# Keys of the cross-attention projected feature-major by head, their inverse roots applied to the scores

## The chip, the cores and the metric

The kernel runs on one core of one Trainium2 chip. The metric is the device time of one launch in microseconds (us). The kernel is written with explicit queues: each engine (PE for matmuls, DVE, ACT, POOL, and SP, which issues DMAs) has its own list of instructions and runs it in order; semaphores order the engines against each other.

## The reference

Input `x` is 16 sequences of 64 rows of 256 floats, and each sequence has a context of 64 rows of 128 floats. All data is float32 except the feed-forward weights and activations after quantising. Three blocks follow each other, each with a residual sum and a layer norm:

1. A chunked linear test-time-training attention (TTT): 16 heads of 16, four chunks of 16 steps. Each chunk needs the state that the chunk before it left, so the four chunks form a chain.
2. A cross-attention with 16 heads of 128 over the context. This is the part that the change touches:

```
q = rmsnorm((x @ Wq).reshape(.., 16, 128), gq)
k = rmsnorm((ctx @ Wk).reshape(.., 16, 128), gk)     # k * rsqrt(mean(k*k) + eps) * gk
attn = softmax(einsum(q, k) / sqrt(128));  out = (attn @ v) @ Wo
```

3. A feed-forward block with weights and activations rounded to 8-bit levels.

## The kernel before, in words

The program has three stages.

**Preparation.** Weights are loaded, transposed, quantised; `x` is transposed and projected for the TTT block; the product of value and output weights of the cross-attention is made (`mvo`).

**TTT stage with the keys between.** DVE runs the chain of four chunks (`chain`, `after_own_terms`, `out_a`, `out_b`, `out_c`, lines 1066 to 1180). PE runs for each chunk `scores_ttt` (L503), `own_terms` (L521) and `state_products` (L511), which are many matmuls of 32 rows and few columns. Between them PE does units of work on the keys of the cross-attention. There are 32 units; a unit is 128 context rows (one main tile) times 512 features (4 heads). PE projects it (L479), which gives the rows token-major. ACT takes four sums of squares (L816) and copies the unit to `kraw` (L817). POOL makes the inverse root and scales the unit (`k_scale`, L1363 to L1365). Three units later PE transposes it head by head (L487), and ACT writes it to `kt` scaled by the gain `gk` (L821). The order is written out by hand: of the units of chunk c (`KEY_UNITS[c]`), PE does the first `FIRST_UNITS[c]` before `scores_ttt(c + 1)`, those up to `EARLY_UNITS[c]` before `own_terms(c)`, and the others behind it, before `state_products(c + 1)`; units 28 to 31 and the last transposes come after the last `own_terms`. ACT has the roots of the chain (L825) between the same units, and POOL the output gating of the chain (L1374 to L1382).

`own_terms(c)` waits for the update of the chunk from DVE (`ub_ready`, L1109). When the last `own_terms` is done (`mg_done` at 8), SP loads `x` a second time (its place had been taken) and the query weights `xwq` (L345 to L348).

**Main loop.** Eight tiles of 128 rows go through a software pipeline (lines 675 to 718 for PE): in iteration i PE projects the queries of tile i (L566), transposes them (L580), makes the scores of tile i (L598, 128 rows by 64 columns of weights, alternately to the upper and lower 64 rows of the output), the context sums and the output of tile i-1 (L610, L618), and the feed-forward of tiles i-2 and i-3 (L637, L647, L655). On DVE the softmax of tile i (L1252 maximum, L1255 subtraction) stands ahead of the rounding of the hidden row of tile i-2 (L1204 to L1208), for whose transposes (`h_transpose`, L647) PE waits at the end of the iteration. The loop starts when the last `o_feat` (L1148) and the last `key_emptied` (L821) are there; its first instruction is `ttt_out` (L661).

## Time and profile before

| | |
|---|---|
| median of 3 runs | 466.35 us (463.65 to 470.18) |
| the profiled execution, span from first to last instruction | 463.8 us |
| PE busy | 373.4 us, 81% |
| DVE busy | 274.3 us, 59% |
| ACT busy | 244.4 us, 53% |
| POOL busy | 218.3 us, 47% |
| preparation, TTT stage, main loop | about 0 to 61, 61 to 207.7, 207.7 to 463.8 us |

For the profiled execution only its span is given; it lies 0.15 us above the fastest run and 2.5 us below the median. Busy shares are means over stages with different limits; what a stage is bound by is read from the waits and the chain inside it. In the slices, each digit is a fortieth of the span (11.6 us).

### The profile page before, as it was taken

The numbers are of one execution on the slowest core, as the hardware profiler recorded it, in microseconds if no ns is written. First come the engines' busy times: TensorE is split into PE (matmuls) and PEld (weight loads), VectorE is DVE, ScalarE is ACT, GpSimd is POOL, SyncE is SP. The second block draws the span as 40 slices with busy tenths as digits, with TensorE's granted clock in tenths as the row PEclk, the third lists the DMA queues.
The fourth block names the chain that finished last, engine by engine and source line by source line (L and its number), as shares of the span: only waits on it lengthen the run. The fifth ranks groups of instructions, "written<-read, shape, count | busy, mean of one in ns | idle before, by whom it ended". The sixth has DMA issues, their size and how long they took to land.

```text
span 463.8 us, 11063 instructions
## 1 busy us (share of the span) xinstructions
PE 373.4 (81%) x4570; PEld 231.0 (50%) x4570; DVE 274.3 (59%) x438; ACT 244.4 (53%) x818; POOL 218.3 (47%) x231
## 2 busy tenths in 40 slices
PE   2999967775775764648869999999999999997952
PEld 2445736444544432424536657485665748464531
DVE  1479953898798895362232427474572737446455
ACT  3036942644453567453655484857568484763320
POOL 2044898699699699761303333232334322224001
PEclk9899975977789979777989999999999999998675
DMA  8990000000000000420000000000000000000000
GB/s 265 193 349 28 0 4 4 6 3 4 3 4 3 3 1 2 171 103 0 2 0 1 0 2 2 11 1 12 2 0 13 1 12 1 11 2 0 13 0 23
DMA packets 12625, 14.54 MB, mean 31 GB/s; under 512 B 2192, under 2 KB 11808, under 8 KB 12064
## 3 DMA queue, kind: packets, MB, share of 16 engines
q1 hardware_dynamic: 12544, 13.83, 9.9%
q8 instruction: 36, 0.59, 0.5%
q14 instruction: 13, 0.11, 0.1%
q10 hardware_dynamic: 32, 0.02, 0.0%
HBM read 12.80 MB, written 1.05 MB: 30 GB/s over the span
## 4 chain that ended last, share of the span: by engine, by line
PE 41%; ACT 6%; DVE 5%; POOL 4%; issue 1%; POOLq 0%; ACTq 0%; DVEq 0%
PE ps L566 12%; PE ps L618 11%; PE ps L610 5%; PE ps L598 3%; PE ps L580 3%; PE ps L637 2%; PE ps L589 2%; PE ps L661 1%; ACT qt L881 1%; PE ps L655 1%; POOL kraw L1365 1%; ACT qjunk L871 1%; POOL krs L1364 1%; ACT cxp L902 1%; PE ps L647 1%
## 5 line engine op out<-in xcount | busy, mean ns | idle before, releaser
L566 PE MATMUL ps<-xwq,x1t 128*128 128x512 f32 x128 | 64.5, 634 | 0.9 <-ACT x1t L893 0.9
L816 ACT ACTIVATE junk<-ps 128x128 bf16<-128x128 f32 x128 | 33.9, 292 | 50.9 <-PE ps L479 50.7
L618 PE MATMUL ps<-mvo,cxp 128*128 128x256 f32 x256 | 58.8, 384 | 0.1
L618 PEld LDWEIGHTS ps<-mvo,cxp 128*128 128x128 f32 x256 | 47.9, 191 | 7.2 <-issue 0.7
L479 PE MATMUL ps<-xwk,ctxt 128*128 128x512 f32 x64 | 46.4, 823 | 0.0
L871 ACT ACTIVATE qjunk<-ps 128x128 f32<-128x128 f32 x128 | 33.4, 279 | 17.9 <-PE ps L566 17.7
L487 PEld LDWEIGHTS ps<-ident,kraw 128*128 128x128 f32 x128 | 18.8, 170 | 46.9 <-issue 23.3
L487 PE MATMUL ps<-ident,kraw 128*128 128x128 f32 x128 | 24.6, 326 | 20.3 <-POOL kraw L1365 9.6
L1365 POOL TENSOR_TENSOR kraw<-kraw,krs 128x512 f32<-128x512 f32 x32 | 36.0, 1126 | 2.5
L1364 POOL TENSOR_TENSOR krs<-krs,mhalf 128x4 f32<-128x4 f32 x32 | 35.5, 1110 | 2.7
L566 PEld LDWEIGHTS ps<-xwq,x1t 128*128 128x128 f32 x128 | 23.2, 198 | 26.6 <-issue 24.0
L1405 POOL TENSOR_SCALAR rstd<-mv 128x1 f32<-128x1 f32 x24 | 5.3, 221 | 58.5 <-DVE mv L1196 58.5
L1422 POOL TENSOR_TENSOR pr<-pr,rq 128x1024 f32<-128x1024 f32 x7 | 13.3, 1902 | 40.7 <-DVE pr L1255 40.7
L1415 POOL TENSOR_SCALAR rq<-qss 128x16 f32<-128x16 f32 x8 | 1.6, 205 | 64.6 <-ACT qtok L872 64.6
L610 PE MATMUL ps<-pt,ctx 64*128 64x512 f32 x64 | 30.2, 698 | 0.7 <-ACT pt L883 0.7
L881 ACT ACTIVATE qt<-ps,gqs 128x512 f32<-128x512 f32 x32 | 22.3, 698 | 13.7 <-PE ps L580 13.7
L816 ACT ACTIVATION_READ_ACCUMULATOR junk<-ps 128x1 f32 x128 | 28.1, 224 | 0.1
L871 ACT ACTIVATION_READ_ACCUMULATOR qjunk<-ps 128x1 f32 x128 | 27.0, 211 | 0.0
L521 PE MATMUL ps<-ak,ub 32*32 32x48 f32 (+1 forms) x1024 | 15.2, 217 | 14.0 <-issue 9.9
L1231 DVE TENSOR_TENSOR rr<-ps,xn 128x256 f32<-128x256 f32 x8 | 3.4, 425 | 38.4 <-PE ps L661 38.4
L821 ACT ACTIVATE kt<-ps,gks 128x512 f32<-128x512 f32 x32 | 23.2, 724 | 4.0 <-PE ps L487 3.9
L1238 DVE TENSOR_TENSOR gs<-ps,s 128x352 f32<-128x352 f32 x16 | 8.4, 525 | 28.5 <-PE ps L637 28.5
(214 smaller groups left out, 849.0 us busy)
## 6 DMA issues: line engine op xcount, KB each, us to landing
xn<-in_x_dram SPq DMA_DIRECT2D x4, 512.0 KB, 4.4
xwo<-in_L_xattn_Wo_dram SPq DMA_DIRECT2D x1, 2048.0 KB, 14.9
xwq<-in_L_xattn_Wq_dram SPq DMA_DIRECT2D x1, 2048.0 KB, 9.2
w1n<-in_L_ffn_w_gate_up_dram SPq DMA_DIRECT2D x1, 1408.0 KB, 9.0
ctx<-in_ctx_dram SPq DMA_DIRECT2D x2, 512.0 KB, 9.2
xwv<-in_L_xattn_Wv_dram SPq DMA_DIRECT2D x1, 1024.0 KB, 12.2
xwk<-in_L_xattn_Wk_dram SPq DMA_DIRECT2D x1, 1024.0 KB, 17.0
out_dram<-x SPq DMA_DIRECT2D x8, 128.0 KB, 1.7
```

What stands on the lines that cost most here:

```text
L479: mm(bank(bk), ctxt[:, i * P:(i + 1) * P], xwk[:, qn * BANK:(qn + 1) * BANK], start=True, stop=True)\
L487: last = nc.tensor.transpose(bank(bk, P, t * P), kraw[:, h * XD:(h + 1) * XD], ident[:, :])
L521: last = mm(ps[part, g * GW + C:g * GW + C + w], ub[part, g * 32:(g + 1) * 32], ak[part, g * (C + 32):g * (C + 32) + w], start=c == 0 and ...
L566: last = mm(bank(n % 2), x1t[:, (i % 2) * D + k * P:(i % 2) * D + (k + 1) * P], xwq[:, k * XH * XD + qn * BANK:k * XH * XD + (qn + 1) * BA ...
L610: turn_done(mm(bank(bk), ctx2[rows, b * CD:(b + 1) * CD], pt[rows, :].rearrange("p (h q) -> p h q", q=P)[:, :, b2 * T:(b2 + 1) * T], start ...
L618: last = mm(bank(6 + turn_of[("y", i, 0)] % 2, D), cxp[:, h * P:(h + 1) * P], mvo[:, h * D:(h + 1) * D], start=h == 0, stop=h == XH - 1)
L816: A(junk[:, t * P:(t + 1) * P], bank(bk, P, t * P), ACT.Square, accum_out=kss[:, h:h + 1])
L821: A(kt[:, m * BANK:(m + 1) * BANK], bank(bk), ACT.Copy, scale=gks[:, 0:1]).then_inc(sem("key_emptied"), 1)
L871: A(qjunk[:, t * P:(t + 1) * P], bank(n % 2, P, t * P), ACT.Square, accum_out=qraw_ss[:, h:h + 1])
L881: ins = A(qt[:, n * BANK:(n + 1) * BANK], src, ACT.Copy, scale=gqs[:, 0:1])
L1364: step(GP.tensor_tensor(krs[:, head], krs[:, head], mhalf[:, 0:4], ALU.pow))
L1365: GP.tensor_tensor(groups(kraw[:, own], XD), groups(kraw[:, own], XD), spread(krs[:, head], 4, XD), ALU.mult)\
```

## The change

The keys are now computed feature-major, one head at a time. A unit is one head (128 features) times 512 context rows (half of them); there are again 32 units. PE's projection has the weights of the head as the stationary side, so that no transposes are needed. ACT squares the unit into `ksq` and copies it to `kt` with the product of both gains. PE sums the squares over the features with a matmul whose stationary side is 32 one-hot columns (`key_sum`): each head adds its sums into a row of its own of PSUM bank 5, even heads in the rows of one group of 32, odd heads in the next. After 16 units ACT takes the roots of 64 rows (`key_roots`). SP writes the rows to DRAM and reads them back in another layout, DVE takes the reciprocal (`key_scales`), SP writes it to DRAM, and for each main tile SP reads a row per sequence, broadcast over the 64 partitions, into `rkb` (two DMAs per tile). In the main loop DVE multiplies the scores by `rkb`, and takes maximum and subtraction from the product. POOL's `k_scale` is gone, and so are the units behind the last `own_terms`.

Some memory moves: `ak` now lies over `ctx2`, so the context is loaded a second time after the last `own_terms`, behind `xwq` and `x`, and PE waits for it before the main loop. The amounts of units ahead of each step change (`KEY_UNITS`, `EARLY_UNITS`). The copy of the transposed queries (L881) has no gain any more.

```diff
-KEY_BANKS, KEY_LAG = 3, 3
-NKU = 4 * NT
-KEY_UNITS = [range(0, 6), range(6, 13), range(13, 20), range(20, 28)]
-TAIL_SPLIT = (2, 4)
+NKU = 2 * XH
+KEY_UNITS = [range(0, 9), range(9, 17), range(17, 25), range(25, NKU + 1)]
 FIRST_UNITS = [3, 2, 2, 2]
-EARLY_UNITS = [4, 5, 5, 8]
+EARLY_UNITS = [7, 7, 7, 8]
...
+        krow0 = place("krow0", BANK)
+        assert cursor[0] == after_kt
+        ak = place("ak", G * (C + 32), over="ctx2")
...
+        krow1 = place("krow1", BANK, over="ctxt")
...
+            def roots_to_rows(half):
+                sp.wait_ge(sem("k_rooted"), half + 1)
+                krow = (krow0, krow1)[half]
+                for odd in range(2):
+                    at = 64 * half + 32 * odd
+                    sp.dma_start(kroot[half].rearrange("b (r o) t -> o r b t", o=2)[odd],
+                                 krow[at:at + XH // 2, :].rearrange("p (b t) -> p b t", t=T)).then_inc(sem("k_rows_out"), 16)
+                sp.wait_ge(sem("k_rows_out"), 32 * (half + 1))
+                sp.dma_start(kinv[:, half * T:(half + 1) * T], kroot[half].rearrange("b h t -> (b h) t")).then_inc(sem("k_roots_in"), 16)
+
+            def scales_out(half):
+                sp.wait_ge(sem("k_inverted"), half + 1)
+                sp.dma_start(kscale[half * B // 2:(half + 1) * B // 2, :].rearrange("b (h t) -> (b h) t", t=T),
+                             kinv[:, half * T:(half + 1) * T]).then_inc(sem("k_scales_out"), 16)
+
+            def scale_rows(i):
+                sp.wait_ge(sem("k_scales_out"), 16 * (i // 4 + 1))
+                if i >= 2:
+                    sp.wait_ge(sem("s_read"), i - 1)
+                for b2 in range(2):
+                    sp.dma_start(rkb[b2 * T:(b2 + 1) * T, (i % 2) * XH * T:(i % 2 + 1) * XH * T],
+                                 kscale[2 * i + b2:2 * i + b2 + 1, :].broadcast_to([T, XH * T])).then_inc(sem("ld_rkb%d" % (i % 2)), 16)
+
+            roots_to_rows(0)
+            scales_out(0)
+            roots_to_rows(1)
             sp.wait_ge(sem("mg_done"), 2 * NCH)
+            load(xwq[:, :].rearrange("p (k n) -> p k n", k=KT), XWq.rearrange("(k p) n -> p k n", p=P), "xwq")
             load_x()
-
-            load(xwq[:, :].rearrange("p (k n) -> p k n", k=KT), XWq.rearrange("(k p) n -> p k n", p=P), "xwq")
+            for half in range(2):
+                load(ctx2[half * T:(half + 1) * T, :].rearrange("p (b c) -> p b c", c=CD), ctx_in.rearrange("b s c -> s b c"), "ctx")
+            sp.wait_ge(sem("k_summed"), NKU)
+            scale_rows(0)
+            scale_rows(1)
+            scales_out(1)
             o = out.rearrange("b t d -> (b t) d")
-            for i in range(NT):
-                sp.wait_ge(sem("x3_ready"), i + 1)
-                sp.dma_start(o[i * P:(i + 1) * P, :], x3[:, (i % 2) * D:(i % 2 + 1) * D]).then_inc(sem("stored%d" % (i % 2)), 16)
+            for i in range(NT + 3):
+                if i >= 3:
+                    t = i - 3
+                    sp.wait_ge(sem("x3_ready"), t + 1)
+                    sp.dma_start(o[t * P:(t + 1) * P, :], x3[:, (t % 2) * D:(t % 2 + 1) * D]).then_inc(sem("stored%d" % (t % 2)), 16)
+                if i + 2 < NT:
+                    scale_rows(i + 2)
...
+            def key_sum(n):
+                half, h = n // XH, n % XH
+                rows = slice(64 * half + 32 * (h % 2), 64 * half + 32 * (h % 2) + 32)
+                pe.wait_ge(sem("k_squared"), n + 1)
+                at = 31 - h // 2
+                mm(bank(5)[rows, :], onehot[:, at:at + 32], ksq[:, (n % 2) * BANK:(n % 2 + 1) * BANK],
+                   start=h < 2, stop=h >= XH - 2).then_inc(sem("k_summed"), 1)
 
...
                 if n < NKU:
-                    i, qn = n // 4, n % 4
-                    bk = key_bank("project", n)
-                    mm(bank(bk), ctxt[:, i * P:(i + 1) * P], xwk[:, qn * BANK:(qn + 1) * BANK], start=True, stop=True)\
+                    half, h = n // XH, n % XH
+                    if n >= 2:
+                        pe.wait_ge(sem("key_emptied"), n - 1)
+                    mm(bank(6 + n % 2), xwk[:, h * XD:(h + 1) * XD], ctxt[:, half * BANK:(half + 1) * BANK], start=True, stop=True)\
                         .then_inc(sem("key_done"), 1)
-                m = n - KEY_LAG
-                if m >= 0:
-                    bk = key_bank("transpose", m)
-                    pe.wait_ge(sem("k_scaled"), m + 1)
-                    for t in range(4):
-                        h = m % 4 * 4 + t
-                        last = nc.tensor.transpose(bank(bk, P, t * P), kraw[:, h * XD:(h + 1) * XD], ident[:, :])
-                    last.then_inc(sem("key_done"), 1)
+                if n >= 2 and n % 2 == 0:
+                    key_sum(n - 2)
+                    key_sum(n - 1)
...
-            for n in range(KEY_UNITS[-1].stop, NKU + KEY_LAG):
-                key_unit(n)
...
-            pe.wait_ge(sem("key_emptied"), len(key_turns))
+            pe.wait_ge(sem("key_emptied"), NKU)
+            pe.wait_ge(sem("k_rooted"), 2)
+            pe.wait_ge(sem("ld_ctx"), 64)
...
+            A(gks[:, 1:2], gks[:, 0:1], ACT.Copy, scale=gqs[:, 0:1]).then_inc(sem("gains"), 1)
...
+            def key_roots(half):
+                act.wait_ge(sem("k_summed"), (half + 1) * XH)
+                rows = slice(64 * half, 64 * half + 64)
+                A((krow0, krow1)[half][rows, :], bank(5)[rows, :], ACT.Sqrt, bias=eps_t[rows, 1:2], scale=1.0 / XD)\
+                    .then_inc(sem("k_rooted"), 1)
...
             def key_unit(n):
...
-                    bk = key_wait("project", n)
-                    if n >= 1:
-                        act.wait_ge(sem("key_emptied"), key_of[("project", n - 1)] + 1)
-                    if n >= 4:
-                        act.wait_ge(sem("key_done"), key_of[("transpose", n - 4)] + 1)
-                    for t in range(4):
-                        h = n % 4 * 4 + t
-                        A(junk[:, t * P:(t + 1) * P], bank(bk, P, t * P), ACT.Square, accum_out=kss[:, h:h + 1])
-                    A(kraw[:, n % 4 * BANK:(n % 4 + 1) * BANK], bank(bk), ACT.Copy).then_inc(sem("key_emptied"), 1)
-                m = n - KEY_LAG
-                if m >= 0:
-                    bk = key_wait("transpose", m)
-                    A(kt[:, m * BANK:(m + 1) * BANK], bank(bk), ACT.Copy, scale=gks[:, 0:1]).then_inc(sem("key_emptied"), 1)
+                    half, h = n // XH, n % XH
+                    act.wait_ge(sem("key_done"), n + 1)
+                    if n >= 2:
+                        act.wait_ge(sem("k_summed"), n - 1)
+                    A(ksq[:, (n % 2) * BANK:(n % 2 + 1) * BANK], bank(6 + n % 2), ACT.Square).then_inc(sem("k_squared"), 1)
+                    if n == XH + 12:
+                        act.wait_ge(sem("k_rows_out"), 32)
+                    o = kt[:, :].rearrange("p (i h t) -> p h i t", h=XH, t=P)[:, h, half * 4:half * 4 + 4]
+                    A(o, bank(6 + n % 2).rearrange("p (i t) -> p i t", t=P), ACT.Copy, scale=gks[:, 1:2]).then_inc(sem("key_emptied"), 1)
+                if n >= XH and n % XH == 0:
+                    key_roots(n // XH - 1)
...
-            rest = range(KEY_UNITS[-1].stop, NKU + KEY_LAG)
-            for n in rest[:TAIL_SPLIT[0]]:
-                key_unit(n)
             root_of(ovs, osd, "ovs_ready", 2 * NCH - 1, "osd_ready")
-            for n in rest[TAIL_SPLIT[0]:TAIL_SPLIT[1]]:
-                key_unit(n)
             root_of(ovs, osd, "ovs_ready", 2 * NCH, "osd_ready")
-            for n in rest[TAIL_SPLIT[1]:]:
-                key_unit(n)
...
-                    ins = A(qt[:, n * BANK:(n + 1) * BANK], src, ACT.Copy, scale=gqs[:, 0:1])
+                    ins = A(qt[:, n * BANK:(n + 1) * BANK], src, ACT.Copy)
...
+                if c == 0:
+                    dve.wait_ge(sem("job_done"), index_of[("ctxt", (1,))] + 1)
...
+            def key_scales(half):
+                dve.wait_ge(sem("k_roots_in"), 16 * (half + 1))
+                own = slice(half * T, (half + 1) * T)
+                V.reciprocal(kinv[:, own], kinv[:, own]).then_inc(sem("k_inverted"), 1)
...
+                if c >= NCH - 2:
+                    key_scales(c - (NCH - 2))
...
                     dve.wait_ge(sem("sc_done"), i + 1)
-                    step(V.tensor_reduce(mx[:, :], groups(s, T), AX.X, ALU.max))
+                    dve.wait_ge(sem("ld_rkb%d" % (i % 2)), 32 * (i // 2 + 1))
                     if i >= 2:
                         dve.wait_ge(sem("tp_done"), tp_of[("pt", i - 2, 1)] + 1)
-                    V.tensor_tensor(groups(z, T), groups(s, T), spread(mx[:, :], XH, T), ALU.subtract).then_inc(sem("s_read"), 1)
+                    V.tensor_tensor(z, s, rkb[:, (i % 2) * XH * T:(i % 2 + 1) * XH * T], ALU.mult).then_inc(sem("s_read"), 1)
+                    dve.wait_ge(sem("s_read"), i + 1)
+                    step(V.tensor_reduce(mx[:, :], groups(z, T), AX.X, ALU.max))
+                    V.tensor_tensor(groups(z, T), groups(z, T), spread(mx[:, :], XH, T), ALU.subtract).then_inc(sem("s_shifted"), 1)
                     if i == 0:
-                        dve.wait_ge(sem("s_read"), 1)
+                        dve.wait_ge(sem("s_shifted"), 1)
                         dve.wait_ge(sem("rq_ready"), 1)
                         V.tensor_tensor(groups(z, T), groups(z, T), spread(rq[:, :], XH, T), ALU.mult).then_inc(sem("z_ready"), 1)
...
+            step(GP.memset(onehot[:, :], 0.0))
+            GP.memset(onehot[:, 31:32], 1.0).then_inc(sem("mask_parts"), 1)
...
-            def k_scale(n):
-                own = slice(n % 4 * BANK, (n % 4 + 1) * BANK)
-                head = slice(n % 4 * 4, (n % 4 + 1) * 4)
-                pool.wait_ge(sem("key_emptied"), key_of[("project", n)] + 1)
-                step(GP.tensor_scalar(krs[:, head], kss[:, head], 1.0 / XD, RMS_EPS, ALU.mult, ALU.add))
-                step(GP.tensor_tensor(krs[:, head], krs[:, head], mhalf[:, 0:4], ALU.pow))
-                GP.tensor_tensor(groups(kraw[:, own], XD), groups(kraw[:, own], XD), spread(krs[:, head], 4, XD), ALU.mult)\
-                    .then_inc(sem("k_scaled"), 1)
...
-                for n in KEY_UNITS[c][:EARLY_UNITS[c]]:
-                    k_scale(n)
...
-                for n in KEY_UNITS[c][EARLY_UNITS[c]:]:
-                    k_scale(n)
-            rest = range(KEY_UNITS[-1].stop, NKU)
-            for n in rest:
-                k_scale(n)
...
-                    pool.wait_ge(sem("s_read"), i + 1)
+                    pool.wait_ge(sem("s_shifted"), i + 1)
```

## Rows read from the trace of the kernel before

**Rows 1.** The page, part 2: granted clock of PE in 40 slices, tenths.
```profile
PEclk9899975977789979777989999999999999998675
```
**Rows 2.** Waits, 60 to 208 us, DVE: total us, times, longest.
```profile
DVE qhR L1113 <- PE ps L521: 15.9, 5, 8.3
DVE ogt L1148 <- POOL oR L1382: 3.6, 2, 2.4
```
**Rows 3.** The page, part 5: busy, mean ns | idle before. POOL's key work.
```profile
L1365 POOL TENSOR_TENSOR kraw<-kraw,krs 128x512 f32<-128x512 f32 x32 | 36.0, 1126 | 2.5
```
**Rows 4.** Line L479: duration ns min/median/max, first and last start us.
```profile
L479 PE MATMUL ps<-xwk,ctxt x64: 592/697/1222, 62.8 to 197.3; 128*128 128x512 f32 x64
```
**Rows 5.** Timeline of PE: start, us, line, count [idle before <-releaser].
```profile
75.96 2.08 PE L479 MATMUL ps<-xwk,ctxt 128*128 128x512 f32 x2
77.83 1.06 PE L487 MATMUL ps<-ident,kraw 128*128 128x128 f32 x4
78.82 4.27 PE L521 MATMUL ps<-ak,ub 32*32 32x48 f32 x256
...
108.99 1.22 PE L521 MATMUL ps<-ak,ub 32*32 32x48 f32 x97 [1.84 <-DVE ub L1109]
...
144.24 2.16 PE L521 MATMUL ps<-ak,ub 32*32 32x48 f32 x177 [2.14 <-DVE ub L1109]
...
182.69 1.13 PE L521 MATMUL ps<-ak,ub 32*32 32x16 f32 x112
```
**Rows 6.** Windows: us, busy of PE, PEld, DVE, ACT, POOL, PEclk, DMA share, GB/s.
```profile
71.00:81.00 10.00, 8.29 (x352) 6.67 (x344) 2.13 (x4) 2.21 (x10) 7.83 (x11) 0.50 0.02 5
```
**Rows 7.** Timeline of PE: four passes of 512 columns; 64 passes of 64 columns.
```profile
291.57 1.88 PE L566 MATMUL ps<-xwq,x1t 128*128 128x512 f32 x4
...
303.35 2.08 PE L598 MATMUL ps<-kt,qt 128*64 128x64 f32 x64
```
**Rows 8.** Line L1101, min/median/max: a DVE step of the chain, with and without POOL.
```profile
L1101 DVE TENSOR_TENSOR uR<-dd,rn x3: 691/1411/1411, 105.2 to 174.8; 128x512 f32<-128x512 f32 x3
```
**Rows 9.** Timelines of PE and DVE in chunk 3.
```profile
168.20 1.11 PE L487 MATMUL ps<-ident,kraw 128*128 128x128 f32 x4 [4.45 <-ACT kraw L817]
...
178.28 0.71 DVE L1109 STREAM_TRANSPOSE ub<-ubt 128x512 f32<-128x512 f32 x1
```
**Rows 10.** Timelines of DVE and PE from the last own terms to the main loop.
```profile
190.48 0.45 DVE L1113 STREAM_TRANSPOSE qhR<-ps 128x256 f32<-128x256 f32 x1 [3.75 <-PE ps L521]
...
197.00 0.35 DVE L1137 RECIPROCAL ors<-osd 128x32 f32<-128x32 f32 x1 [2.55 <-ACT osd L825]
...
204.72 0.71 DVE L1148 STREAM_TRANSPOSE ogt<-oR 128x512 f32<-128x512 f32 x1
...
207.68 3.54 PE L661 MATMUL ps<-wo,ogt 128*128 128x256 f32 x8 [0.87 <-ACT kt L821]
```
**Rows 11.** DMA issues: KB each, median us to landing; last row: `ctx` alone.
```profile
xwq<-in_L_xattn_Wq_dram SPq DMA_DIRECT2D x1, 2048.0 KB, 9.2
ctx<-in_ctx_dram SPq DMA_DIRECT2D x2, 512.0 KB, 9.2
out_dram<-x SPq DMA_DIRECT2D x8, 128.0 KB, 1.7
...
DMA to landing us min/median/max: 7.9/9.2/10.5
```
**Rows 12.** Windows, as in rows 6: the second load of `x` and `xwq`.
```profile
193.00:200.00 7.00, 5.83 (x24) 2.76 (x22) 4.24 (x7) 7.00 (x37) 5.42 (x8) 0.94 1.04 408
```
**Rows 13.** Timelines of DVE and PE in main tiles 0 and 3.
```profile
237.65 1.50 PE L589 MATMUL ps<-ident,pr 128*128 128x128 f32 x8 [4.18 <-DVE pr L1270]
...
308.47 1.22 DVE L1255 TENSOR_TENSOR pr<-ps,mx 128x1024 f32<-128x1024 f32 x1
...
312.15 0.53 DVE L1208 TENSOR_SCALAR hq<-gs 128x704 bf16<-128x704 f32 x1
...
312.74 0.63 PE L647 MATMUL ps<-ident_b,hq 128*128 128x128 bf16 x6
```

48 lines of the change are left out of this document (20 added, 28 removed).

## The prediction

> **What bounds the kernel now.** I read the clock by slice first, then the waits of DVE, then the timelines of PE and DVE stage by stage. From slice 22 on the clock is full until the last tiles, and in the TTT stage (slices 6 to 18) it wavers between seven and nine tenths [rows 1], since PE pauses there. So there are two regimes. In the TTT stage DVE runs the chain of four chunks, and what holds it is mostly PE's `own_terms`: 15.9 us of waits, of which 8.3 in chunk 0; POOL holds it for 3.6 us [rows 2]. In the main loop PE sets the pace, unless a result that it needs comes late. One is on the edge: in tile 3 the rounded hidden row ends at 312.68 (312.15 + 0.53) and PE's transposes of it start at 312.74 [rows 13]; the same pair of rows stands so in each of tiles 2 to 5, and with 0.36 us to spare in tile 6. This edge and the stretch between the last update and the main loop decide the case; the shares of busy time don't.
>
> **What POOL's relief is worth.** `k_scale` vanishes, 36.0 us in its scaling alone [rows 3]. POOL is no bound, so this counts only where it held others. A DVE step of the chain takes 691 or 1411 ns, and the long ones lie beside a POOL instruction [rows 8]. Beside key instructions lie one such step in chunk 1 on the way to the update (0.7 us), one in chunk 2 (0.7), and 1.2 us in chunk 3; behind `own_terms(2)` there are 1.3 us more, and about 1.8 us of the wait for the gated output [rows 2], which then starts without a key unit ahead of it.
>
> **What the key units cost on PE.** Before, a unit was one product of 512 columns (two passes) and four transposes, 2.08 and 1.06 us at half clock (a pass takes 592 ns at the full level of 2.4 GHz and up to 1222 at 1.2) [rows 4, 5]. Passes of 512 columns follow each other every 0.47 us at full clock (1.88 / 4) [rows 7], with the key pattern's small gaps 0.51, so a product is 1.02. After, a unit has one product and one one-hot sum, also 512 columns. The trace has no such sum. Its nearest row is L598, whose weights of 64 columns write alternately to two halves of the output: 64 passes of 64 columns in 2.08 us, where the rate of L566 would give 3.8 (4096 x 0.92 ns) [rows 7]. So two column groups overlap. A pair of sums (four passes) costs 1.02 us if all overlap, 2.04 if none do. I take 1.43, three pass slots, since passes start in order and the second sum's first pass can only lie beside the first sum's last. Two units are then 3.5 us of PE against 3.3 before.
>
> After L598 PE goes on with full-width weights with no gap above 0.1 us in the timeline, so I price the change of shape at 0. The Trainium skill (TensorEngine Tiling (Array Packing), Key Properties) says instead that changing the tiling mode drains the engine, which speaks against a scheme that changes it twice for each of 16 pairs; by that rule with 0.2 us for a drain, an estimate, the stage would be up to 6 us longer, and most of that would lie ahead of `own_terms`. It belongs to the slower rival below.
>
> **Chunk by chunk**, the shift of `own_terms` against before:
> - Chunk 0. Before, unit 3 alone stood ahead: 75.96 to 78.82, at half clock [rows 5, 6], with the update long there. Now units 3 to 6: four products and two pairs, 4 x 1.02 + 2 x 1.43 = 6.9 us of full-speed work. The clock stays at half to about 81.2 as before, where the window at 0.50 ends [rows 6], in which 5.2 us do 2.6 of it; the other 4.3, with gaps of 0.3, end at 85.8. Shift +7.0 (bounds +4.4, all at full clock, and +8.2, no overlap).
> - Chunk 1. DVE's update comes at +7.0 - 0.7. PE has five units ahead (five products, two pairs, 8.3 us) against 7.0 us for three units before, plus 2.6 for a half-clock stretch as long as the one there. So PE ends last: +8.6 on 108.99 [rows 5]. Behind it stands one unit instead of two, -0.6.
> - Chunk 2. The same count ahead: +8.9 on 144.24. Behind it DVE ends last, with 3.2 us less (the relief above, less 0.5 for the new reciprocal): the state is read at +5.7.
> - Chunk 3. The update, before at 178.3, comes at +5.7 - 1.2 = 182.8. Units 26 to 31 wait, as before [rows 9], for ACT, which stands at a root of the chain; from there 9.2 us of units and 2.5 for the half clock give 185.3 against 182.69 before, which POOL paced. Shift **+2.6**, bounds -1 (update alone) and +5.
>
> **From the last own terms to the main loop.** Before: SP issues the loads at 190.5, and the main loop starts at 207.7 [rows 10], 17.2 us, held by the last key units. These go. Then two things race. DVE's tail was 190.48 to 205.43; without the key units on ACT ahead of the root the wait of 2.55 becomes the usual 0.39, one step loses 0.7 of contention, and the reciprocal adds 0.5: 12.8 us. The loads: `xwq` and `x` ran at 408 GB/s with the DMAs full [rows 12] and ended 10.2 us after `own_terms` (issued 1.0 later, 9.2 to landing [rows 11]). The context adds 1 MB behind them in 512 B pieces. In the preparation its halves were issued 0.7 us apart and took 7.9 and 10.5 to landing [rows 11], so the second ended 3.3 after the first, and the first 2.6 after the transfer ahead of it. That makes +5.9: 16.1 us. Bounds 12.8 (1 MB at 408 GB/s is 2.5 us) and 17.5. So the context takes the place of the key tail, and **1.1 us** of 17.2 are gained.
>
> The reciprocal of the second half waits for a trip through DRAM: root 0.9 us after the last unit, two writes and a read issued at 0.5 each, two landings of 1.7 [rows 11], 5.5 us in all. Covered by `own_terms(3)`, which takes 7.7; if it took the 4.3 of chunk 0 [rows 5], DVE would wait 1 us, and the context would still hide it. SP has its wait for those writes ahead of the big loads, done some 3 us before they are due. In the main loop the rows for tile i+2 are asked for when tile i's scores are read, over 27 us ahead of need, and stores wait behind them for nothing later; cost 0.
>
> **Main loop.** DVE gets one more instruction of 128x1024 per tile, 1.22 us [rows 13], 1.26 with its hand-over. In tiles 2 to 5 it lies in front of the rounding, whose chain has no slack: 4 x 1.26, in tile 6 0.9. In tile 0 PE waits for the softmax as it is (4.18 us [rows 13]), and in tile 7 too: 2 x 1.26. Tile 1 has 1.3 us to spare: 0.1. Sum 8.6. The copy of the queries without a gain takes 0.61 instead of 0.69 and stands on the path once per tile or twice: -0.8. So **+7.8**; bounds 2.7 (tiles 2 to 6 hidden) and 10.
>
> **Sum.** 463.8 + 2.6 - 1.1 + 7.8 = 473.1 us of span. The page's span lies at the fastest run and 2.5 us below the median; I put the median at 474.
>
> **Rivals.**
> 1. Slower: sums that do not overlap or that drain PE, at half clock. Place: ahead of `own_terms`. Each pair costs 0.6 to 1 us more; two pairs ahead in chunks 0 to 2, three behind the root in chunk 3; some 8 pairs, 5 to 8 us, nearly doubled while the clock is at 1.2 GHz, less what DVE's slack takes. It decides from where `own_terms` starts right behind a sum rather than behind the update. For it: the clock [rows 6]; against it L598. 473.1 + 7 = 480.
> 2. Faster: denser PE work keeps the clock up (for it: the old half-clock stretches follow pauses; against it: those pauses are the small matmuls, which stay). Then the update alone holds chunk 3 at -1 to -3, and the context comes with the first bound: 473.1 - 5 - 2.5 = 465.5.
> 3. The multiplication is hidden, since ACT and DVE drift apart from PE by a tile: 473.1 - 5 = 468. Against it: four tiles show the same 0.06 us.
> 4. The roots don't come in time (the trip is longer than its cover), so DVE waits ahead of `out_a(3)` and the tail starts late: each us beyond 2 counts once the context is passed; 477. Little for it.
> 5. Much faster, under 457: needs 2 and 3 together and more.
>
> **Chances.** Forecast (470 to 476) 0.40, rival 1 0.22, rival 2 0.15, rival 3 0.10, rival 4 0.06, rival 5 0.07. The time is 474, the range 462 to 482. A measurement here tells about 2% from no change, 457 to 475.7. The forecast lies across the upper bound, nearer inside: two thirds of it, rivals 2, 3 and a third of 4 count as same, 0.54; rival 1, the rest of the forecast and of 4 as slower, 0.39; faster 0.07.
>
> **What would show it.** In the timeline of PE: pairs of sums in 1.4 us at full clock; `own_terms` at about 86, 118, 153 and 185. The main loop's first product behind a wait for the context, about 209. Between the last output product of tile i-1 and the transposes of the hidden row (tiles 2 to 5) an idle time of about 1.2 us with DVE as releaser, and a tile period of 28.3 instead of 27.1. I am wrong if `own_terms(3)` starts before 181, if the loop starts behind `o_feat` and not the context, or if the period stays at 27.1.

## The result, and the profile after

The changed kernel takes 468.19 us (median of 4 runs, 467.75 to 468.77) against 465.39 us (463.65 to 470.18), ratio 1.0128 [1.0083, 1.0173]: somewhat slower, within the 2%. The ratio is that of the fast runs; the plain quotient of the two medians is 1.006. 474 was forecast with a range of 462 to 482. The profiled run has a span of 466.3 us (time 468.09), 2.5 over the 463.8 of before, where 473.1 was forecast. In the four runs of the changed kernel the span is 1.7 to 1.9 us shorter than the time of the same run; so a span should not be compared with other runs' times, as it was when the median was forecast, and 473.1 us of span stands for about 475 of time. The small difference hides two large movements of opposite sign, which the positions of `own_terms` and of the loop show (us in the span; the loop's start is the first product of `ttt_out`):

| | own 0 | own 1 | own 2 | own 3 | loop start | last scores | span |
|---|---|---|---|---|---|---|---|
| before | 78.8 | 109.0 | 144.2 | 182.7 | 207.7 | 411.1 | 463.8 |
| forecast | 85.8 | 117.6 | 153.1 | 185.3 | 209.2 | | 473.1 |
| after | 82.6 | 114.7 | 145.0 | 175.4 | 199.6 | 409.8 | 466.3 |

The loop starts 8.1 us earlier, not 1.5 later, and then takes 266.7 us instead of 256.1, not 263.9. Of the 8.1, 1.75 were there already in the preparation, which has no work on the keys (the first scores of the TTT stage started 1.75 earlier; the first 16 products of the preparation took 7.1 us instead of 8.8, a half-clock stretch being shorter).

The clock by slice, from the page. Against [rows 1], counting slices from 0: higher in slices 6, 8 to 10, 14 and 18, lower in 13 and 15, and 0.5 in slices 16 and 17, where it was 0.7.
```profile
PEclk9999977988889787559899999999999999996685
```
Windows (columns as [rows 6]), first before, from `own_terms(0)` to `own_terms(3)` chunk by chunk:
```profile
78.82:108.99 30.17, 22.16 (x811) 15.15 (x811) 25.31 (x33) 18.47 (x79) 24.28 (x24) 0.85 0.01 4
108.99:144.24 35.25, 24.02 (x811) 16.28 (x811) 29.46 (x41) 16.30 (x74) 29.63 (x30) 0.81 0.01 3
144.24:182.69 38.45, 24.59 (x572) 14.68 (x572) 31.68 (x44) 22.10 (x102) 33.10 (x36) 0.87 0.01 2
```
and after:
```profile
82.60:114.68 32.08, 25.03 (x804) 12.18 (x803) 25.56 (x36) 12.01 (x21) 7.57 (x5) 0.89 0.01 3
114.68:144.96 30.28, 23.32 (x801) 11.60 (x800) 25.83 (x37) 10.48 (x21) 10.63 (x7) 0.89 0.03 6
144.96:175.37 30.41, 24.12 (x549) 9.89 (x549) 27.06 (x42) 11.39 (x22) 8.26 (x6) 0.83 0.01 4
```
PE is busy 1.7 us more than before, POOL 60 us less in the three. DVE runs the same chain in 8.0 us less busy time, all of it in the second and third, and sits idle 3.1 us less. Its waits after, 57 to 200 us, answer to [rows 2]:
```profile
DVE qhR L1145 <- PE ps L555: 15.6, 3, 12.8
DVE ogt L1180 <- POOL oR L1417: 2.5, 2, 1.2
```
The wait for own terms has the same sum, but now 12.8 of it in chunk 0. The steps of the chain that ran beside POOL are at their short time, where [rows 8] had 1411:
```profile
L1133 DVE TENSOR_TENSOR uR<-dd,rn x3: 691/691/692, 108.1 to 171.7; 128x512 f32<-128x512 f32 x3
```
The timeline of PE after. L518 is the product of a unit, L508 the sum of squares, x4 being two units, a pair of heads; L555 `own_terms`, L693 `ttt_out`, L679 the transposes of the hidden row in tile 3. It answers to [rows 5, 10, 13].
```profile
80.57 1.12 PE L518 MATMUL ps<-ctxt,xwk 128*128 128x512 f32 x2 [0.27 <-ACT kt L856]
81.62 1.05 PE L508 MATMUL ps<-ksq,onehot 128*32 128x512 f32 x4
82.60 1.63 PE L555 MATMUL ps<-ak,ub 32*32 32x48 f32 x130
...
173.57 1.87 PE L508 MATMUL ps<-ksq,onehot 128*32 128x512 f32 x4
175.37 1.50 PE L555 MATMUL ps<-ak,ub 32*32 32x16 f32 x152
179.01 1.06 PE L555 MATMUL ps<-ak,ub 32*32 32x16 f32 x104 [2.13 <-issue]
199.61 3.75 PE L693 MATMUL ps<-wo,ogt 128*128 128x256 f32 x8 [19.54 <-DMA ctx<-in_ctx_dram]
...
303.84 3.62 PE L650 MATMUL ps<-mvo,cxp 128*128 128x256 f32 x16
308.70 0.63 PE L679 MATMUL ps<-ident_b,hq 128*128 128x128 bf16 x6 [1.24 <-DVE hq L1247]
```
Four things to see: a pair of sums takes 1.05 us at full clock (1.92 at half clock, at 151.47) and the full-width products on both sides follow without a gap; `own_terms(3)` follows right behind a pair, which takes 1.87 us although the clock is full, since its second sum starts at 174.39 only, when ACT has squared the last unit (below); the loop stands 19.5 us behind a DMA; and PE waits 1.24 us for the hidden row, as forecast. ACT ahead of that pair's second sum:
```profile
173.74 0.60 ACT L852 ACTIVATE ksq<-ps 128x512 f32<-128x512 f32 x1
```
On DVE in tile 3:
```profile
301.91 1.23 DVE L1294 TENSOR_TENSOR pr<-ps,rkb 128x1024 f32<-128x1024 f32 x1
...
308.12 0.53 DVE L1247 TENSOR_SCALAR hq<-gs 128x704 bf16<-128x704 f32 x1
```
SP's queue behind the last own terms, start and time of each issue:
```profile
180.12 0.40 SPq L318 DMA_DIRECT2D xwq<-in_L_xattn_Wq_dram  x1
180.56 2.54 SPq L318 DMA_DIRECT2D xn<-in_x_dram  x2
183.15 6.30 SPq L318 DMA_DIRECT2D ctx<-in_ctx_dram  x2
189.56 5.60 SPq L366 DMA_DIRECT2D rkb<-kscale  x4
```
The engines meanwhile (columns as [rows 6], the last three PEclk, DMA share and GB/s):
```profile
180.00:208.00 28.00, 6.93 (x20) 3.98 (x14) 13.85 (x26) 1.03 (x3) 2.06 (x5) 0.51 0.74 190
```
DVE had the last features written at 191.95; PE waits 7.7 us beyond that, and its clock is at the lower level, 1.2 GHz.

### The profile page after: what moved, and what is told of

It is laid out like the page before. It is cut to its first block, busy times and chain, and to the rows that moved or that the text cites. A ratio compares the mean times of both kernels' runs of the same rounds, so it can differ in the third digit from the quotient of the medians.

```text
span 466.3 us, 10600 instructions
## 1 busy us (share of the span) xinstructions
PE 371.8 (80%) x4506; PEld 214.4 (46%) x4506; DVE 276.9 (59%) x448; ACT 210.1 (45%) x565; POOL 134.2 (29%) x137
## 3 DMA queue, kind: packets, MB, share of 16 engines
q1 hardware_dynamic: 16768, 19.27, 15.3%
## 4 chain that ended last, share of the span: by engine, by line
PE 46%; DVE 26%; ACT 8%; POOL 7%; issue 6%; DMA 4%; SPq 2%; POOLq 0%; DVEq 0%; ACTq 0%
PE ps L598 12%; PE ps L642 5%; PE ps L429 4%; PE ps L518 4%; PE ps L650 3%; DMA ctx<-in_ctx_dram 3%; PE ps L612 3%; PE ps L508 2%; PE ps L621 2%; SPq L318 2%; DVE pr L1294 2%; DVE mx L1296 2%; DVE pr L1297 2%; PE ps L669 2%; ACT sg L942 2%
## 5 line engine op out<-in xcount | busy, mean ns | idle before, releaser
L518 PE MATMUL ps<-ctxt,xwk 128*128 128x512 f32 x64 | 45.6, 829 | 4.4 <-ACT kt L856 3.5
L852 ACT ACTIVATE ksq<-ps 128x512 f32<-128x512 f32 x32 | 19.1, 596 | 61.1 <-PE ps L518 33.4
L901 ACT ACTIVATE qjunk<-ps 128x128 f32<-128x128 f32 x128 | 33.6, 281 | 16.1 <-PE ps L598 15.9
L911 ACT ACTIVATE qt<-ps 128x512 f32<-128x512 f32 x32 | 19.2, 602 | 14.7 <-PE ps L612 14.7
L693 PE MATMUL ps<-wo,ogt 128*128 128x256 f32 x32 | 9.9, 447 | 19.5 <-DMA ctx<-in_ctx_dram 19.5
L518 PEld LDWEIGHTS ps<-ctxt,xwk 128*128 128x128 f32 x64 | 13.4, 243 | 25.8 <-issue 14.4
L1444 POOL TENSOR_TENSOR rq<-rq,mhalf 128x16 f32<-128x16 f32 x8 | 23.3, 2910 | 0.7
L612 PEld LDWEIGHTS ps<-ident,qtok 128*128 128x128 f32 x128 | 15.4, 141 | 16.4 <-issue 13.0
L923 ACT ACTIVATE x1t<-ps 128x256 f32<-128x256 f32 x8 | 3.1, 384 | 42.7 <-PE ps L701 42.7
L932 ACT ACTIVATE cxp<-ps 128x512 f32<-128x512 f32 x32 | 18.9, 628 | 6.9 <-PE ps L642 6.9
L537 PE MATMUL ps<-kq,kb 32*32 32x16 f32 x1024 | 11.4, 186 | 12.3 <-issue 10.0
## 6 DMA issues: line engine op xcount, KB each, us to landing
xwv<-in_L_xattn_Wv_dram SPq DMA_DIRECT2D x1, 1024.0 KB, 12.8
```

Source lines behind the costliest of these rows:

```text
L518: mm(bank(6 + n % 2), xwk[:, h * XD:(h + 1) * XD], ctxt[:, half * BANK:(half + 1) * BANK], start=True, stop=True)\
L612: last = nc.tensor.transpose(bank(bk, P, t * P), qtok[:, (n % 2) * BANK + t * P:(n % 2) * BANK + (t + 1) * P], ident[:, :])
L852: A(ksq[:, (n % 2) * BANK:(n % 2 + 1) * BANK], bank(6 + n % 2), ACT.Square).then_inc(sem("k_squared"), 1)
L901: A(qjunk[:, t * P:(t + 1) * P], bank(n % 2, P, t * P), ACT.Square, accum_out=qraw_ss[:, h:h + 1])
L911: ins = A(qt[:, n * BANK:(n + 1) * BANK], src, ACT.Copy)
L932: freed(A(o, bank(bk).rearrange("p (h q) -> p h q", q=T), ACT.Copy))
```

## The experiments

Ratios are against the kernel before. In the profiled runs of the changed kernel's variants, the first and the fourth below excepted, the TTT stage begins 1.5 to 3 us later than in that of the changed kernel itself (the first transposed update stands at 70.9 to 72.5 us instead of 69.44; in the kernel before at 71.17); I call this the offset, and take it off where a start is compared. The stage also differs between runs in which only the main loop was edited: measured from the first transposed update, `own_terms(2)` stands at 75.1 to 78.8 us in the five runs with the changed kernel's stage (75.5 in the changed kernel itself, 73.1 in the kernel before). A shift of 1 or 2 us between two single traces is therefore no effect by itself.

**The wait for the context** (PE's wait moved from ahead of the loop to the first product that reads it):
```
-            pe.wait_ge(sem("ld_ctx"), 64)      # ahead of the loop
+                if i == 0 and n == 0:          # in context_sum(i, n)
+                    pe.wait_ge(sem("ld_ctx"), 64)
```


> The changed kernel with one wait moved: PE waits for the second load of the context before the first context sum (tile 0, some 36 us into the loop) and no longer ahead of the loop. Theory A (the context reload alone holds the start of the loop: DVE's tail ended at 191.95 us, the loop began at 199.6): the loop starts at about 192.3, when x is there, and the span falls from 466.3 to 458.9 (-7.4). Rival (x and the query weights, which share the DMAs, are as late, or PE only meets a colder clock): the start moves by less than 2 us and the span stays above 464.


460.6 us, 0.9959 [0.992, 0.9997], span 458.3. The loop starts at 192.61, 7.0 earlier, held by DVE:
```profile
192.61 3.78 PE L695 MATMUL ps<-wo,ogt 128*128 128x256 f32 x8 [11.93 <-DVE ogt L1181]
```
So the late landing cost 7.0 us at the loop's start; the context itself is not waited for at its new place. The loop is another 1.0 us shorter, in its tail, where the clock differs (see the main loop below).

**No multiplication of scores** (L1294 left out; the maximum and the subtraction read PSUM as before, so the keys' roots reach no score):
```
-                    V.tensor_tensor(z, s, rkb[...], ALU.mult).then_inc(sem("s_read"), 1)
-                    step(V.tensor_reduce(mx[:, :], groups(z, T), AX.X, ALU.max))
+                    step(V.tensor_reduce(mx[:, :], groups(s, T), AX.X, ALU.max))
```


> The changed kernel with the multiplication of the scores by rkb left out: maximum and subtraction read PSUM as before the change; the DMAs of rkb and the wait for them stay. The scores lack the keys' inverse roots, so the output is another. Theory A (the loop is longer by one DVE instruction ahead of the rounding of the hidden row): the loop falls from 266.7 to 256 us, the tile period from 28.26 to 27.0, PE's idle time ahead of the transposes of the hidden row from 1.24 to 0; span 456 to 457. Rival (the rkb DMAs or their wait cost the time): the period stays above 28 and the span above 464.


459.0 us, 0.9898 [0.981, 0.9986], span 459.1. The period is 27.0, PE's wait for hidden rows in tiles 2 to 5 is gone, and the loop takes 258.0 us instead of 266.7.

**The same multiplication in the kernel before:**
```
+                    step(V.tensor_tensor(groups(z, P), groups(s, P), ones..., ALU.mult))
-                    step(V.tensor_reduce(mx[:, :], groups(s, T), AX.X, ALU.max))
+                    step(V.tensor_reduce(mx[:, :], groups(z, T), AX.X, ALU.max))
```


> The kernel before, with one thing of the change: in the main loop VectorE multiplies a tile's 128x1024 scores by ones from PSUM into the buffer that the softmax uses, and the maximum and the subtraction read the product. Theory A (this multiplication alone makes the main loop's loss of 10.6 us, by the hidden rows' wait in six tiles and by the tail): loop 265 to 267 us instead of 256.1, span 472 to 474, TensorE waits 1.2 us for hidden rows in tiles 2 to 5. Theory B (the loss has another part, such as the scale rows' loads, or the tail's clock): loop under 262, span under 469.


474.15 us, 1.0207 [1.0122, 1.0292], span 474.3. The loop starts at 207.69, as before to 0.01 us, and ends 10.5 us later; the wait has moved in as in the changed kernel:
```profile
317.73 0.63 PE L647 MATMUL ps<-ident_b,hq 128*128 128x128 bf16 x6 [1.24 <-DVE hq L1208]
```
Taken out of one kernel and put into the other, this one instruction a tile is worth 8.7 and 10.5 us of the loop's 10.6. With it left out the loop still takes 1.9 us more than before; the rows' loads may have up to that.

**Hidden rows transposed a tile later** (ahead of the down products that read them):
```
-                if last2:
-                    h_transpose(i - 2)         # behind the output products
...
+                if last3:
+                    h_transpose(i - 3)         # behind q_quarter(i, 0)
                 if cur:
                     q_quarter(i, 1)
+                if last3:
+                    ffn_down(i - 3)
```


> The changed kernel with PE's transposes of the hidden row moved behind the first query projection of the next iteration, and the down projection behind the second; ACT's copy likewise. All work is kept. Theory A (only the place of these transposes makes the multiplication cost anything in tiles 2 to 6): the period falls from 28.26 to about 27.1, 5.8 us in all; tiles 0 and 7 keep their 1.8 and 1 to 3.8; span 460.5. Rival (PE then waits at the next thing, the softmax for its transposes, which has 1.4 us of room, or the copy delays the squares of the queries by up to 0.9 us a tile): period 27.9, span 464 or more.


461.94 us, 0.9983 [0.995, 1.0016]; the period falls to 26.9 with the multiplication in place, the loop takes 261.1, 5.6 less. Of the 10.6 some 5 stay, in tile 0, where PE waits for the softmax itself (5.54 us, 4.18 in the kernel before), and in the tail.

**POOL's load put back.** With each key unit, POOL runs an add and a power over 128x4 and two multiplications over 128x256 into a spare buffer, in the places of `k_scale`:
```
+            def pool_load(n):
+                if n < NKU:
+                    pool.wait_ge(sem("key_emptied"), n + 1)
+                    step(GP.tensor_scalar(pool_pad[:, 0:4], ones[:, 0:4], 1.0 / XD, RMS_EPS, ALU.mult, ALU.add))
+                    step(GP.tensor_tensor(pool_pad[:, 4:8], pool_pad[:, 0:4], mhalf[:, 0:4], ALU.pow))
+                    for part in range(2):
+                        step(GP.tensor_tensor(pool_pad[:, 0:256]..., xwk[:, 0:256]..., ones..., ALU.mult))
```


> The changed kernel with a dummy load on POOL in the TTT stage in the place of k_scale: per key unit one 128x4, one 128x4 power and two 128x256 multiplications that read SBUF; nothing waits for its results. Theory A (2.4 of the some 5 us by which DVE's chain from state read to update is shorter than before come from POOL's key instructions, the rest from where POOL's other work falls; together the relief is 5 us over three chunks, and the wait for the gated output about 1.3): the last own terms end at 184 to 187 instead of 180.1, span 470 to 473. Rival (the stage is shorter through PE and its clock, and POOL was no bound): the last own terms within 1.5 us of 180.1, span 466 to 468.


485.8 us, 1.0471 [1.04, 1.0543], span 484.0: the loop starts at 218.1, 18.5 later (16.4 without the offset), beyond both. The waits of DVE, 60 to 218 us:
```profile
DVE ogt L1181 <- POOL oR L1418: 25.1, 3, 9.7
```
At 2.8 to 4.0 us a unit the padding filled POOL's queue and held the gated output. A lighter load, with one multiplication a unit:

> The changed kernel with less of the key normalization's old POOL load put back than in the run with two scaling steps a unit: for each of the 32 units an add over 128x4, a power over 128x4 and one multiplication over 128x256, into a spare buffer, about 2.3 us a unit instead of 3.6. In the heavier run the loop began 18.5 us late; 25 us of VectorE's time went in three waits for POOL's gated output (9.7 us the longest), which stands behind seven units in POOL's queue. Theory A (POOL's load costs by its queue: the gated output stands behind it): with 2.3 us a unit the seven units fit before the output scale is wanted, the waits for POOL fall under 6 us in sum, and the loop begins 2 to 6 us late: span 468 to 472. Theory B (it costs by contention of POOL with VectorE, in proportion to POOL's busy time): 60% of the heavier run's loss, 10 to 11 us: span 477.


476.43 us, 1.0256 [1.0176, 1.0337], span 477.6, loop start 212.5: 12.9 later, 11.4 without the offset. The wait for POOL is 9.5 us (over 57 to 212):
```profile
DVE ogt L1181 <- POOL oR L1418: 9.5, 2, 5.1
```
The number is near B's, yet contention is not what it shows: DVE was busy 79.5 us from own terms 0 to 3, against 78.5 without the load, and the step that [rows 8] had at 1411 ns kept its 691. So this load costs by the queue (and the roots' trip through DRAM, for which DVE waits 2.1 us here). The segments of the stage tell where (us; "read" is the first transpose of the state product, "update" the first transposed half):

| | before | after | light load | heavy load |
|---|---|---|---|---|
| own 1 to read 2 | 16.5 | 14.0 | 17.4 | 22.5 |
| read 2 to update 2 | 17.9 | 15.0 | 15.3 | 16.2 |
| own 2 to read 3 | 16.5 | 14.0 | 18.3 | 22.5 |
| read 3 to update 3 | 16.2 | 15.0 | 15.4 | 16.3 |
| update 3 to own 3 | 5.7 | 1.4 | 2.0 | 0.9 |

The gated output lies in the own-to-read rows, and there any POOL work comes back. The read-to-update rows (1.2 to 2.9 us shorter after) come back only by 0.3 to 1.3. The padding has no 128x512 instruction. It also leaves POOL's output gating in its new place: in chunk 2 the gating starts 0.2 us behind the state's read in the changed kernel and in both padded runs, 3.2 us behind it in the kernel before, where it lay beside the DVE steps L1088 and L1090 (1.52 and 1.63 us, now 0.69 each).

The two runs show that POOL's queue can hold the chain. They don't show how much it held before: the padding stands seven units deep ahead of the output's last steps, `k_scale` stood five deep, and all of DVE's waits for the gated output were 3.6 us then and are 2.5 now.

**All sums in one column group** (both parities of a pair to the same 32 columns):
```
-                rows = slice(64 * half + 32 * (h % 2), 64 * half + 32 * (h % 2) + 32)
-                at = 31 - h // 2
+                rows = slice(64 * half, 64 * half + 32)
+                at = 31 - h
```
(The rows then go out in one DMA for each half instead of two, and the root takes 32 rows.)


> The changed kernel, but the sums of squares of both heads of a pair go to the same 32 columns of TensorE (16 rows used instead of 8 and 8), so that a pair of sums can't run side by side. Theory A (the pair measured 1.0 us at full clock because the two 32-column sums run beside each other): a pair becomes 1.7 to 2.0 us, 32 pairs add 25 to 30 us of TensorE in key projection, and as some of it stands in TensorE's slack behind VectorE the stage ends 4 to 10 us later: 470 to 476. Theory B (the pair is quick for another reason, and column groups do nothing): pair 1.0 us, time 466 to 468.


470.65 us, 1.0111 [1.007, 1.0151], span 467.8. The same pair, first here, then in the changed kernel:
```profile
99.91 1.90 PE L507 MATMUL ps<-ksq,onehot 128*32 128x512 f32 x4
```
```profile
99.00 1.05 PE L508 MATMUL ps<-ksq,onehot 128*32 128x512 f32 x4
```
So the two groups do run fully side by side. Yet doubling the sums moves the loop's start by only 3.0 us, 1.3 without the offset, and the span by 1.5: under the 4 to 10 that theory A gave, and within what runs with the same stage differ by (with only the hidden rows moved, the loop starts at 201.95). There are 16 pairs, not the 32 of the expectation: at 0.9 us each PE has 14 us more, and nearly all of it lay behind DVE.

**Both schedule edits together** (the context's wait and the later hidden transposes):

> The changed kernel with both edits tried singly before: TensorE waits for the second context only ahead of tile 0's first weighted sum of the context, and a tile's hidden rows are transposed one tile later, ahead of its down products. Theory A (the two gaps are independent: a late landing that costs 6 to 7 us once, and 1.2 us a tile for a VectorE that now takes 1.3 us more ahead of the hidden rows): the two gains add, 466.3 - 8.0 - 5.6 = 452.7 us of span, period of a tile 27.0, 2% under the kernel before. Theory B (they share a limit, TensorE at half clock or VectorE full after the stage, so that one gain eats the other): 457 to 459, as the first edit alone.


456.27 us, 0.9826 [0.9758, 0.9895], span 453.6: theory A to 1 us, with the offset in it. The interval lies clear of 1 and reaches across the 2% line.

**The later transposes in the kernel before:**

> The kernel before with the one scheduling edit of the combined version that applies to it: a tile's hidden rows are transposed one tile later (it has no second load of the context). Theory A (the hidden rows stood 0.06 us ahead of TensorE, so before there is nothing to win there; the later place only pays once VectorE has the extra multiplication): period 27.0 to 27.1, span 463 to 465, same as before, and the combined version's lead of 2% needs the change. Theory B (the later place is a gain of its own): span 458 to 461, and about half of the lead has nothing to do with the change.


464.1 us, 1.001 [0.998, 1.004]: nothing (the time alone; period and span of this run are not compared). The edit pays only with the multiplication there, and the other one has no place in the kernel before, which loads no second context.

**Key units moved out of chunk 0** (on the combined version; 7, 9, 9, 7 a chunk):
```
-KEY_UNITS = [range(0, 9), range(9, 17), range(17, 25), range(25, NKU + 1)]
-EARLY_UNITS = [7, 7, 7, 8]
+KEY_UNITS = [range(0, 7), range(7, 16), range(16, 25), range(25, NKU + 1)]
+EARLY_UNITS = [5, 7, 7, 8]
```


> The combined version (span 453.6), with two of chunk 0's nine key units moved out of it: 7, 9, 9 and 7 units a chunk instead of 9, 8, 8, 7; five instead of seven stand ahead of the own terms of chunk 0. Theory A (VectorE's wait of 12.8 us for the own terms of chunk 0 is on the chain, and chunks 1 and 2 have room in TensorE behind VectorE for one more unit each): own terms of chunk 0 at 80 instead of 84.7, loop start 3 to 5 us earlier, span 449 to 451. Theory B (TensorE has no room left in chunks 1 and 2, so that the work comes back there): own terms of chunk 0 earlier, those of chunks 2 and 3 where they were, loop start within 1 us of 196.4, span 453 to 455.


450.51 us, 0.9678 [0.9633, 0.9723], span 448.8, the fastest here. The loop starts at 189.8, 6.7 earlier, more than A had. Own terms 0 start 1.8 earlier (82.94; the update ended 1.0 later in this run), own terms 1 4.9 and own terms 3 7.0. And two more to the last chunk (5, 9, 9, 9):

> As the run with 7, 9, 9 and 7 key units a chunk (span 448.8, VectorE still waits 10.1 us for the own terms of chunk 0), with two more units moved out of chunk 0, to the last one: 5, 9, 9 and 9, of which three stand ahead of the own terms of chunk 0. Theory A (that wait is still on the chain, and chunk 3 has room in TensorE): own terms of chunk 0 some 3 us earlier, loop start 1 to 3 us earlier, span 446 to 448. Theory B (the last chunk, whose units all stand ahead of its own terms, has no room for two more): own terms of chunk 3 start as late as before or 2 to 4 us later, span 449 to 453.


452.2 us, 0.9799 [0.9749, 0.9849], span 450.5. Own terms 0 start at 76.0, but now those of chunk 2 wait for PE, and those of chunk 3 start 4.0 later than with 7, 9, 9, 7. PE and, below, DVE in chunk 2:
```profile
143.57 1.05 PE L508 MATMUL ps<-ksq,onehot 128*32 128x512 f32 x4
144.55 1.65 PE L555 MATMUL ps<-ak,ub 32*32 32x48 f32 x135
```
```profile
138.87 0.71 DVE L1142 STREAM_TRANSPOSE ub<-ubt 128x512 f32<-128x512 f32 x1
...
146.13 0.35 DVE L1176 RECIPROCAL ors<-osd 128x32 f32<-128x32 f32 x1 [3.93 <-ACT osd L863]
```
The first half of the update is done at 139.6, the own terms stand 5.0 us later behind a key unit. In chunk 3 they stand 3.0 us behind it. So B's effect came where B put it, and one chunk earlier as well.

## Why the forecast held in its class and missed in its steps

**The sum came nearer than its parts.** The stage was forecast 9.6 us too late, the loop 2.8 too short; the difference is the 6.8 us of span. That the second error took something off the first is luck. The 1.75 us from the preparation are chance too, and went against the forecast.

- **Chunk 0**, +7.0 forecast. Measured +3.8, of which -1.75 from the preparation: +5.5 of its own. Right in kind (TensorE ends last, DVE waits 12.8). The pair of sums was mis-sized, 1.43 forecast, 1.05 measured: 0.8 us for the two pairs at full clock. The value at the nearest row, which showed full overlap, was the better one. The rest is the clock, which was back at the full level from 78.1 us on (0.50 from 74.35 to 78.10, 0.97 from there to 82.60), not from 81.2. By the same pair the Trainium skill's drain at a change of tiling mode (TensorEngine Tiling (Array Packing), Key Properties) has no visible price here: the full-width product ahead of a pair and the work behind it follow without a gap in the rows above. The 0.2 us that the prediction tried for a drain had no row behind it.
- **Chunk 1**: right. TensorE ends last, 3.7 us behind the first half of the update (done at 111.00), and from own terms 0 to own terms 1 it is 32.1 us where 31.8 were forecast.
- **Chunk 2**, the step that failed: "The same count ahead: +8.9 on 144.24", which carries the lateness of chunk 1 on. Measured 144.96; from own terms 1 to own terms 2 the forecast was 0.3 more than before, measured 5.0 less. The lateness against before shrinks inside the round: 5.7 us at own terms 1, 1.3 at the end of TensorE's state product, 1.9 where DVE has transposed it, 0.3 at the update, 0.7 at own terms 2. So 4.4 us come back in TensorE's own queue. `own_terms(1)` took 5.6 us instead of 8.3: before, TensorE had paused for the update ahead of it and ran the larger part of it at half clock; now it comes from key units without a pause. And the units behind it take 3.2 us instead of 5.2, where the forecast had 0.6 for the one unit less. Before and after (columns as [rows 6]):
```profile
112.57:117.20 4.63, 3.59 (x160) 3.28 (x160) 2.42 (x4) 0.00 (x0) 4.13 (x4) 0.50 0.03 5
```
```profile
114.68:117.30 2.62, 2.58 (x223) 2.44 (x223) 1.00 (x3) 1.55 (x4) 0.60 (x1) 1.00 0.03 6
```
Another 1.6 us come from DVE's steps between the state and the update; I had one step of 0.7 there. The wait that DVE had for the state product before is gone:
```profile
127.21 0.45 DVE L1080 STREAM_TRANSPOSE khR<-ps 128x256 f32<-128x256 f32 x1 [1.35 <-PE ps L511]
```
How much comes back varies. In the changed kernel's trace `own_terms(2)` starts 0.6 us after the first half of the update is done. In three other traces of the same stage (no multiplication, hidden rows later, both edits) TensorE is 3.4 to 4.8 us behind it, as the prediction had it in kind, and own terms 1 to 2 takes 32.9 to 34.3 us instead of 30.3; in the run with the hidden rows later the clock was 0.75 over the 13.9 us ahead of `own_terms(2)`, in the changed kernel 0.88. Measured from the first update, the forecast for `own_terms(2)` is 81.9 us, 3.1 to 6.9 too late in all five.
- **Chunk 3**: 185.3 forecast, 175.4 measured. Of the 9.9, 1.75 come from the preparation, 1.5 from chunk 0, 5.3 from the step above, and 1.7 from here; 0.3 goes the other way, in chunk 1. The 1.7 are TensorE's last units: from the wait for ACT at 165.93 to `own_terms(3)` 9.4 us, where the forecast had 11.7, less 0.6 by which the state's read came later than forecast. The prediction named `own_terms(3)` before 181 as its refutation, and that is what came.
- **POOL's relief** was mis-sized by less. Behind `own_terms(2)` 3.2 us were forecast (its own terms, 1.3 + 1.8 - 0.5, give 2.6) and 2.5 measured; 1.2 forecast and 1.2 measured in the update of chunk 3; 0.7 forecast and 1.6 measured in that of chunk 2. DVE's busy time fell by 8.0 in all. The load put back shows that a queue ahead of the gated output can hold the chain. DVE steps stretched beside POOL's 128x512 are seen in the rows of before (below) and gone after, but no run put that instruction back alone: how much of the 8.0 it makes, and how much the new place of the output gating, is argued, not shown.
- **Last own terms to the loop**: 23.9 us forecast, 24.2 measured, from two terms that were off. `own_terms(3)` took 4.7 instead of 7.7, and the context landed 19.4 us after it instead of 16.1 (bounds 12.8 to 17.5, so outside). SP stood 2.54 us at the issue of `x` and 6.30 at that of `ctx`; the row loads (1 MB), priced at 0, were issued from 189.56 on and ran beside the context. No run separates the two. The place of the wait was right, and the first experiment shows it was the whole of it.
- **Root trip**: covered, as forecast, with 0.6 us to spare: the read was issued at 178.19 and took 1.7 to landing, and DVE's reciprocal at 180.50 follows its predecessor at once. With the light load on POOL it was not covered (2.1 us of wait).
- **Main loop**: mechanism right (1.24 us of wait in tiles 2 to 5, period 28.26), the size under: +10.6 against +7.8. Tile 0 cost 1.8 instead of 1.26, and the tail 3.8 instead of 1.26. In the tail, the copy in the kernel before made 2.0 of that. The other 1.8 go with the clock from 24 to 32 us behind the last scores. It is 0.60 in the four traces with a tail of 56.3 to 56.5 us (the changed kernel, hidden rows later, one column group, light load) and 0.80 to 0.84 in the six others with the multiplication, whose tail is 54.7 to 55.0 us. In the changed kernel, and with the context's wait moved:
```profile
433.80:441.80 8.00, 7.89 (x24) 4.89 (x23) 5.37 (x10) 2.77 (x4) 0.00 (x0) 0.60 0.00 0
```
```profile
427.34:435.34 8.00, 7.89 (x32) 5.16 (x31) 5.37 (x10) 2.77 (x4) 0.00 (x0) 0.80 0.00 0
```
In all four the loop began behind the context, in none of the six; so the tail's 1.8 us may belong to that wait too, but how it would reach so far is not shown.
- **A reading**: slice 6 of [rows 1] is 5, not "between seven and nine tenths"; it is the stretch that the prediction prices at half clock all the same.

Of the rivals, rival 2 was nearest in the stage, and its reason, that denser TensorE work keeps the clock up, is what `own_terms(1)` shows (0.81 to 0.89 in the second window). But `own_terms(3)` came 7.3 us earlier, not 1 to 3, and it did not get its early context; that its 465.5 lies next to the span of 466.3 is luck. Rival 1 falls with the pair at 1.05 us, rival 3 with the 1.24 us, rival 4 with the reciprocal.

## What to carry to other kernels

A shift at one step is not carried through to the next round of a chain: here 5.7 us shrank to 1.3 inside one engine's queue, since less work and a higher clock stood behind it. Redo the whole round on the assumption that each engine might end last. Load on an engine that is not the bound costs where its queue stands ahead of something the bound engine needs. An instruction put ahead of a handover with 0.06 us of slack costs its full time each tile, unless the consumer is moved by a tile, which cost nothing here. A wait for an input that is only read later belongs at its reader; and after a gain in balance, the work between chunks has to be dealt out again, which here was worth another 5 us.

## What the hardware showed that I had not expected

- Two sums of 512 columns on 32-column groups took 1.05 us side by side and 1.90 in one group, both at full clock.
- SP's issue of two context halves (512 KB each) took 6.30 us and that of four row loads 5.60, while the DMAs were busy; the issue of `xwq` ahead of them took 0.40. The issue of `x` took 2.54 us behind `xwq` and 0.93 in the kernel before, where it stood first.
- While PE waited for the context its granted clock was 0.51, and it was 0.50 in the first 8 us of the loop (0.71 in the kernel before, which had no such wait). This cost nothing there: the first scores come 19.0 us after the loop's start, 19.2 before.
- Whether a DVE step is stretched depends on who came first. In the kernel before, POOL's scaling was running when DVE's step began, and the step took 1.41 instead of 0.69, and POOL's 1.40 instead of 1.04 (POOL, then DVE):
```profile
139.92 1.40 POOL L1365 TENSOR_TENSOR kraw<-kraw,krs 128x512 f32<-128x512 f32 x1
```
```profile
140.46 1.41 DVE L1101 TENSOR_TENSOR uR<-dd,rn 128x512 f32<-128x512 f32 x1
```
With the light load DVE's step was ahead, and kept its time, while POOL's took 0.97 instead of 0.61 (POOL, then DVE); so padding that starts behind DVE's steps costs DVE nothing:
```profile
148.43 0.97 POOL L1425 TENSOR_TENSOR pool_pad<-xwk,ones 128x256 f32<-128x256 f32 x1
```
```profile
148.24 0.69 DVE L1134 TENSOR_TENSOR uR<-dd,rn 128x512 f32<-128x512 f32 x1
```
